# Four one-column products in place of one 128x4 product in both norms of the second layer

## What is computed

```
def _layernorm(x, w, b):                       # at the end of the first layer's attention
    mu = jnp.mean(x, axis=-1, keepdims=True)
    var = jnp.mean((x - mu) ** 2, axis=-1, keepdims=True)
    return (x - mu) * jax.lax.rsqrt(var + LN_EPS) * w + b

x = x + _L0_attn_ref(xn, ...) + _L0_ffn_ref(xn, ...)
xn = _layernorm(x, axis=-1)                    # ahead of the second layer
x = x + _L1_attn_ref(xn, ...) + _L1_ffn_ref(xn, ...)
```

## Time and profile before

| | |
|---|---|
| median of three runs | 784.57 us (782.51 to 787.86) |
| the profiled execution | 784.8 us, of which its span is 783.1 us |
| mean granted clock of TensorE | 0.991 of full speed |
| PE busy | 724.7 us, 93% |
| DVE busy | 730.3 us, 93% |
| POOL busy | 645.4 us, 82% |
| ACT busy | 587.2 us, 75% |

### The profile page before, as it was taken

The page is one execution under the profiler, slowest core; times in us unless marked ns, Lnnn a source line. Parts: engine busy times, 40 slices in busy tenths (PEclk is TensorE's granted clock), DMA queues, the critical chain, the costliest instruction groups (busy, mean ns, idle before and its releaser), DMA issues.

```text
span 783.1 us, 13328 instructions
## 1 busy us (share of the span) xinstructions
PE 724.7 (93%) x3457; PEld 526.1 (67%) x3457; DVE 730.3 (93%) x2036; ACT 587.2 (75%) x1363; POOL 645.4 (82%) x640
## 2 busy tenths in 40 slices
PE   4999986599999999999999999787889999999998
PEld 3555543478878888888888888652456666656655
DVE  5999999899999999999999999997798898899987
ACT  6888886689798888889988898775655556657631
POOL 3687889797888989979898798768898788989873
PEclk9999999799999999999999999999999999999999
DMA  5677866601612326161161251512422212120011
GB/s 128 208 259 247 276 225 198 148 15 28 136 40 67 81 64 124 41 147 41 41 147 41 52 96 42 158 39 61 160 82 82 68 41 69 55 70 25 1 28 41
DMA packets 139242, 75.77 MB, mean 97 GB/s; under 512 B 74922, under 2 KB 123052, under 8 KB 139180
## 3 DMA queue, kind: packets, MB, share of 16 engines
q1 hardware_dynamic: 138124, 74.58, 34.4%
q10 hardware_dynamic: 1056, 0.52, 0.2%
HBM read 39.86 MB, written 33.55 MB: 94 GB/s over the span
## 4 chain that ended last, share of the span: by engine, by line
PE 58%; POOL 9%; DVE 7%; ACT 3%; issue 3%; DMA 1%; SPq 0%; DVEq 0%; POOLq 0%; ACTq 0%
PE f_ps L2295 13%; PE f_ps L2297 8%; PE f_ps L2431 7%; PE f_ps L2432 6%; PE f_ps L2302 5%; PE f_ps L2331 5%; PE f_ps L2408 4%; POOL f_g L1552 2%; POOL f_gl L1544 2%; PE r_rec L2460 2%; PE r_rec L2466 1%; DVE l_qs L1347 1%; DVE r_rec L1273 1%; PE r_rec L2450 1%; POOL f_hl L1544 1%
## 5 line engine op out<-in xcount | busy, mean ns | idle before, releaser
L1674 POOL TENSOR_TENSOR l_kv<-l_qkv 128x1024 f32<-128x1024 f32 x64 | 124.5, 1949 | 18.3 <-PE f_ps L2432 18.2
L1273 DVE TENSOR_REDUCE r_rec<-r_pg 128x32 f32<-128x288 f32 x256 | 114.6, 448 | 0.6 <-ACT r_pg L1893 0.6
L1285 DVE TENSOR_REDUCE r_gain<-r_kw 128x64 f32<-128x256 f32 x256 | 103.8, 406 | 0.0
L2295 PE MATMUL f_ps<-f_gh,w_hi 128*128 128x512 f32 x256 | 100.0, 391 | 1.4 <-POOL f_gl L1544 1.3
L1544 POOL TENSOR_TENSOR f_hl<-f_h,f_hh 128x512 fp32r<-128x512 f32 x64 | 80.8, 1291 | 24.0 <-ACT f_hh L1939 23.6
L2295 PE MATMUL f_ps<-f_hh,w_hi 128*128 128x512 f32 x256 | 99.9, 390 | 0.0
L1347 DVE TENSOR_TENSOR l_qs<-f_ps,l_qd 128x1024 f32<-128x1024 f32 x64 | 78.2, 1221 | 22.3 <-PE f_ps L2432 15.9
L1552 POOL TENSOR_TENSOR f_g<-f_a,f_b 128x512 f32<-128x512 f32 x64 | 82.1, 1292 | 16.8 <-ACT f_b L1928 16.8
L1544 POOL TENSOR_TENSOR f_gl<-f_g,f_gh 128x512 fp32r<-128x512 f32 x64 | 82.4, 1299 | 0.0
L1354 DVE TENSOR_REDUCE l_o_in<-l_qs 128x128 f32<-128x1024 f32 x64 | 77.2, 1211 | 0.6
L2297 PE MATMUL f_ps<-f_hl,w_hi 128*128 128x512 f32 x192 | 74.8, 389 | 0.0
(11 more groups left out here) (231 smaller groups left out, 2124.6 us busy)
## 6 DMA issues: line engine op xcount, KB each, us to landing
scratch_xnT<-p_xnT SPq DMA_DIRECT2D x16, 256.0 KB, 2.8
scratch_K<-p_kout SPq DMA_DIRECT2D x16, 256.0 KB, 2.3
scratch_fac<-p_fac SPq DMA_DIRECT2D x16, 256.0 KB, 2.3
scratch_R<-p_rr SPq DMA_DIRECT2D x16, 256.0 KB, 2.3
scratch_P<-p_pp SPq DMA_DIRECT2D x16, 256.0 KB, 3.1
first_x<-scratch_xnT SPq DMA_DIRECT2D x16, 256.0 KB, 3.6
first_xt<-in_L_attn_x_dram SPq DMA_DIRECT2D x16, 256.0 KB, 3.0
scratch_W<-r_w SPq DMA_DIRECT2D x16, 256.0 KB, 4.1
```

Source lines behind the costliest of these rows:

```text
L1273: dve.tensor_reduce(w_here(g, blk), pg[q][:, at, :, :, :].rearrange("p (v g) i k -> p v g i k", g=G)[:, :, g, :, :], AX.X, ALU.add).then_i ...
L1285: dve.tensor_reduce(of_group(g, gain), of_group(g, kw), AX.X, ALU.add).then_inc(gain_ok, 1)
L1674: pool.tensor_tensor(dst, k, v, ALU.mult).then_inc(kv_ok, 1)
L2295: nc.tensor.matmul(bank, c.w_hi[:, weights[k], :], upper[k], start=k == 0, stop=False)
```

## The change

`nm1` and `nm2` are made one column at a time. `tensor_tensor` and `scalar_tensor_tensor` on 128x4 (for unit 3 on 128x3) become four (three) `tensor_scalar` instructions on 128x1, in which the inverse root is the scalar per partition. The semaphore rises with the last of them, as before with the only one. Nothing else is changed.

```
-            dve.tensor_tensor(nm1[:, cols(u)], mean1[:, cols(u)], rs1[:, cols(u)], ALU.mult).then_inc(nm1_ok, 1)
+            for b, t, i in tiles(u):
+                ins = dve.tensor_scalar(nm1[:, i:i + 1], mean1[:, i:i + 1], rs1[:, i:i + 1], None, ALU.mult)
+            ins.then_inc(nm1_ok, 1)
@@
-            dve.scalar_tensor_tensor(out=nm2[:, cols(u)], in0=mv2[:, cols(u), 0], scalar=-1.0, in1=rs2[:, cols(u)],
-                                     op0=ALU.mult, op1=ALU.mult).then_inc(nm2_ok, 1)
+            for b, t, i in tiles(u):
+                ins = dve.tensor_scalar(nm2[:, i:i + 1], mv2[:, i, 0:1], rs2[:, i:i + 1], -1.0, ALU.mult, ALU.mult)
+            ins.then_inc(nm2_ok, 1)
```

## The result

| | kernel before | changed kernel |
|---|---|---|
| median | 786.59 us (782.51 to 787.86, 5 runs) | 781.19 us (780.33 to 782.12, 5 runs) |
| ratio, 95% interval | | 0.9941 (0.9917 to 0.9965) |
| profiled execution, span | 784.8 us, 783.1 us | 782.1 us, 780.4 us |
| instructions on DVE | 2036 | 2118 |

Two more runs of the kernel before raised its median from 784.57 to 786.59 us. Run once more, the changed kernel came out at 779.9 us against 786.85 us, a ratio of 0.9917 (0.9897 to 0.9937). The intervals overlap.

A forecast was written before the change was run, and what follows sets the result against it. PE was taken to set the pace in regular rounds, so gain lay in irregular places where PE waits for a held product. Terms summed to -3.9 us, from 784.8 to 780.9, stated as 780.8 us; range 776.5 to 787.0.

The forecast's parts named there:

- The price of the new instruction: Each one-column instruction takes 0.21 us, one every 0.12 us; a group of four 0.57 us, bounds 0.31 to 0.85.
- No column waits for POOL: Assumed for all new 128x1 instructions: reading one tensor and a scalar per partition is not held by POOL.
- 554.59 and 564.66: Two products at these times (us) get shorter and PE loses waits: -0.45 and -0.25 us.
- 578.45: Product held 4.16 us becomes 0.57; PE's idle 2.59 us and the clock loss go: -3.0 us (-2.1 to -4.4).
- 694.29: Product of 1.70 us becomes 0.57 and PE's 0.64 us wait for L1347 goes: -0.6 us (0 to -0.64).
- 738.60: Product not held before, so what stands behind it comes 0.40 us later: +0.4 us (0 to +0.75).
- The gain doesn't arrive: Rival, 784.5 us: column pace near the upper bound, or POOL stays late after 578 us; chance 0.24.
- Each column held by itself: Rival: four instructions wait for POOL where one did; at most 160 us, about 865 us if half arrives; chance 0.08.

The follow-up runs named there:

- e8: Changed kernel with the products made by columns on ACT, plus one 128x4 ACT instruction per scale2, DVE making only reciprocals: median 784.14 us, ratio 0.9969 to the kernel before.
- e7: Changed kernel with each group of columns made twice, the first into tiles nobody reads: median 786.06 us, ratio 0.9991 to the kernel before.
- e5: Changed kernel with columns reading two SBUF tensors of one element each instead of a scalar per partition: 803.59 us in one run.
- e6: Changed kernel with scalar-per-partition products on 128x4 (scale1) and 128x3 plus one column (scale2), for time only: 788.74 us in one run.
- e10: Changed kernel with the 128x4 product kept at scale1 of units 4 and 16: median 780.51 us, ratio 0.9922 to the kernel before.
- e3: Kernel before with only scale1 of unit 6 made by columns, one product of 28: median 782.87 us, ratio 0.9945.
- e2: Kernel before with only the scale2 products made by columns, scale1 keeping its wide product: median 784.58 us, ratio 0.9965.
- e4: Changed kernel with the 128x4 product put back for scale1 of unit 6 alone: median 784.31 us, ratio 0.9962 to the kernel before.

## Why the prediction held, point by point

- **The time and the sign.** 780.8 us was forecast and 781.19 measured, within the range. That the figures are so close is partly luck. Against its own kernel before the change brought 5.4 us by the first medians and 6.5 by the lengths, and the sum said 3.9. It was set against a profile of before that was about 2 us better than the median of the later runs, and the two errors nearly cancel. By its own sum it should have said 780.7 (784.57 less 3.9), and the low end of the range 776.8 (778.8 less 2); neither matters.
- **What bounds the kernel.** PE sets the pace of the regular rounds: their period did not change (14.36 us), though DVE's lines there got 0.4 us longer and 0.1 us shorter. `e8` shows it best, with the same period and DVE freer by two groups; `e7` shows that DVE would set it with one more group for each.
- **The price of the new instruction.** 0.21 us, one every 0.12 us, 0.57 us for a group and 0.48 us of DVE; measured 0.205, 0.12, 0.58 and 0.49. L1293 was the right row to go by. In `e5` the groups of four that nothing holds take 0.37 us at 0.15 each, one every 0.07 us, so the form with a scalar per partition costs about 0.05 us more per instruction. The Trainium skill ("Vector Engine (DVE) Microarchitecture Reference", section "Measured stream behaviour on trn2") has about 75 ns per instruction after overlap, as an estimate 0.30 us for four. `e5` agrees with its 0.07; for the new instruction the measured 0.49 decides.
- **No column waits for POOL.** Right in the outcome, but the step to it was not sound, and that it held was in part luck. The prediction went from L1293, whose tensors are in PSUM and SBUF, and the reciprocal to "a product that reads two SBUF tensors is held ...; one that reads one tensor isn't". `e6` reads one SBUF tensor and a scalar per partition and is held up to 4.04 us. Had the change used the scalar form on more than one element, the same reasoning would have failed.
- **554.59 and 564.66.** -0.70 forecast together; the gain at the start of unit 6's product is 0.8.
- **578.45.** This term was mis-sized: -3.0 forecast, with -4.4 as its end. From 0.8 to 5.25 us, 4.45 us were gained: 3.0 for the hold and 1.4 for the clock, by the table above, where the prediction's end had 2.6 and 1.8. The step that failed is "What is late next is POOL ... only these 2.1 us can be given back along POOL". POOL did come forward by 2.0 us only: its next `l_kv` starts 9.70 us after the product before (578.45 to 588.15) and 7.71 us after it now. But PE was not waiting for that one. Rows of the kernel before, and then of the changed kernel:

```profile
589.60 1.02 PE L2431 MATMUL f_ps<-l_kv,tri 128*128 128x512 f32 x2
...
593.74 1.02 PE L2431 MATMUL f_ps<-l_kv,tri 128*128 128x512 f32 x2
```

```profile
581.43 0.57 DVE L1321 TENSOR_SCALAR l_nm<-l_mean,l_rs 128x1 f32<-128x1 f32 x4
...
588.06 1.09 PE L2434 MATMUL f_ps<-l_kv,tri 128*128 128x512 f32 x2
...
589.14 1.94 POOL L1677 TENSOR_TENSOR l_kv<-l_qkv 128x1024 f32<-128x1024 f32 x1
...
592.26 1.02 PE L2434 MATMUL f_ps<-l_kv,tri 128*128 128x512 f32 x2
```

  `l_kv` of 588.15 was ready at 590.10, and PE's L2431 for it ran at 593.74: 3.6 us in reserve. In the changed kernel it is ready at 591.08 and used at 592.26, 1.2 us in reserve. An idle time of POOL was read as a limit on PE; what counts is how long its result lies ready before it is used.
- **694.29.** -0.6 forecast, 0.87 us gained.
- **738.60.** +0.4 forecast. Between the marks 0.66 us are lost, in two places: at this product PE waits 0.53 us for L1350 where it waited 0.23 for L1347, and `e10` gets 0.37 back by leaving it wide; the rest goes at 723.55, where PE waits 0.52 us for L1350 and did not wait before. No term had that one.
- **Not foreseen:** about 0.35 us each at two places, near the seventh store (94.94 to 109.66 us against 89.64 to 104.01) and near the thirteenth. At both PE no longer waits for L1347, 0.27 us at 656.71 and 0.18 at 750.91 in `before`, two of the seven waits of the earlier trace rows that the sum passed over. Both are gone as well in `e3`, whose products there have their form of before, and in `e6`, whose form is held too, so it isn't the columns at these places that bring it; what does stayed open.
- **The rivals.** "The gain doesn't arrive" needed a dearer column; `e7` shows that at twice the price it would have nearly come true. "Each column held by itself" is a real mechanism, for columns with two tensors (`e5`), but its price was far too high: 15.8 us over the kernel before, not 80, since no group has more than two held columns and 8 of 28 have none.

## What to carry to other kernels

Where a tiny VectorE instruction has a spread from 0.16 us to several microseconds, compare its ends with those of GpSimd's instructions. If they coincide, changing its operands (here: one element and a scalar per partition) can free it; fewer elements or another opcode alone did not do it here. Then price each hold by what PE waits behind it: of 28 products one gave two thirds of the gain, and the 1.1 us hold right behind it cost nothing. When asking what is late next, look at how long the other engine's result lies ready before it is used, not at whether that engine is idle.

## What the runs showed of the hardware

- A VectorE instruction that waits for POOL doesn't always get in where one POOL instruction ends and the next begins: at unit 6 it was held through `l_qd` and both `l_kv` in all four profiles (4.16 to 4.37 us), and at 694.29 it got in between the two `l_kv`. What decides that stayed open.
- A `tensor_scalar` on 128x4 or 128x3 in fp32 from SBUF to SBUF is held by POOL (up to 4.04 and 1.70 us; 0.23 us when free), on 128x1 it isn't (0.199 to 0.218 us in all runs).
- PE's idle time doesn't tell by itself whether the granted clock falls: 2.59 and 2.61 us of waiting in the two profiles of before were followed by a clock of 0.51 and 0.52 and L2431 pairs of 1.81 and 1.90 us, while 2.46 us in `e6`, 2.76 in `e2` and 2.80 in `e4` were followed by pairs of 1.10 us. What differs ahead of it was not settled.
